# The first expert layer of a two-layer attention and mixture-of-experts kernel computed on rows sorted by expert instead of on all rows

## The chip, the cores and the metric

One core of a Trainium2 chip runs the whole program. The time is microseconds of device time per execution; the profile is one execution of the same program, taken by the hardware profiler.

## The reference

2048 tokens (32 sequences of 64) of 128 channels pass through two layers, each a cross attention of 16 heads followed by a feed-forward with 8 experts of which each token uses 2. All in fp32.

```python
x = x + xattn0(layernorm(x), ctx, ctx, ...)      # 16 heads of 8, keys and values from ctx
x = x + ffn0(layernorm(x), ...)
x = x + xattn1(layernorm(x), ctx, ctx, ...)
x = x + ffn1(layernorm(x), ...)

def ffn0(x, w_gate, w_g, w_u, w_d):              # 8 experts, hidden width 176, top 2
    top, idx = top_k(x @ w_gate, 2)
    gating = sum(one_hot(idx, 8) * softmax(top)[..., None], axis=-2)
    hidden = silu(x @ w_g[e]) * (x @ w_u[e])     # for every expert e
    return sum_e gating[e] * (hidden[e] @ w_d[e])
# ffn1: the same routing, gelu(x @ W1[e] + b1[e]) @ W2[e] + b2[e], hidden width 512
```

## The kernel before

The program is written by hand for each engine: the order of instructions on an engine is the order of the code, and engines meet only through semaphores (`wait_ge`, `then_inc`). Tokens lie in 16 row tiles of 128 (`TILES`), or 4 groups of 4 tiles (`GROUPS`, `G`). Products that need fp32 are made of three fp16 matmuls on high and low halves (`three`): ScalarE writes the high half (names ending in `_high`), VectorE or GpSimd subtracts it to get the low half (`_low`).

Stages in order of time. Setup: weights and context are loaded by SP, turned by TensorE, split; ScalarE fills the ninth column of the values (`vals`, L435 and L436), GpSimd clears the odd keys (L707) and VectorE the even ones (L864). Keys, values, queries of layer 0 follow; SP copies the keys into place (`place_keys`, L346) and TensorE waits for them by `kd0` (tiles 0 to 3) and `kd1` (the rest).

Attention (`attention(l)` on every engine) is a software pipeline of steps `t` from -3 on: in step t the scores of tile t+3 and their maxima (VectorE L1026), the exponentials of tile t+2, the turned probabilities of tile t+1, the weighed values of tile t, the output and residual of tile t-1 and the layer-norm statistics of tile t-2 are made. In layer 0 a step from 1 to 12 also splits one twelfth of the weights of the first feed-forward (`split_high` L477, `chunk0_low` L1224). While it runs SP fills 16,384 rows of a table in device memory, `sorted_rows`, with filler rows (L383 to L387).

First feed-forward before the change. Near the end of the attention rows are normalised and turned in five parts (`PARTS`), the logits ranked (`rank` L1286), and after it `routing` makes a matrix of token by expert weights, `combT`. `experts0` then computes all 8 experts for all tokens: 44 steps (`N0`) of 128 hidden columns by 512 tokens; in each TensorE makes gate and up (6 matmuls of 512 columns), spreads `combT` over the hidden columns (L1796) and adds 12 matmuls of 128 columns to a sum in PSUM; ScalarE applies SiLU (L589) and writes the high half (L593), VectorE multiplies twice (L1276, L1315), GpSimd makes the low half (L815). `residual0` adds a finished group to x and takes its statistics; GpSimd normalises it. In the same loop 8 chunks of the weights of the second feed-forward are split (`CHUNK_STEPS`; L600, and L1321 in two halves each). The projections of layer 1 follow, values and queries mixed (`VALUES_AT`).

Second feed-forward, as it is before and after. During attention 1 each row tile is normalised (L539), turned, its logits taken (`turn_row`, `row_logits`), the two experts chosen (`choose`), ranks within each expert counted by TensorE (`part_ranks`) and the row's place in `sorted_rows` found (`locate`), in five parts (`SORT_PARTS`). GpSimd scatters every row twice (`scatter` L784, 32 indirect DMAs), each expert's rows one after another. A table of 23 slot tiles (`MT`) of 256 rows says which expert and which rows each has: 5 (`MT0`) are found from the first 12 row tiles (`early_tiles`), 18 from all (`late_table`). `experts1` loads a slot tile (SP L411, four buffers), turns it (L1816, two transposes), splits it (L609, L1349), makes 12 matmuls of 256 columns and 26 of 128, GELU between them, and GpSimd stores the results by token into `expert_sums` (L835, two indirect DMAs a tile, eight buffers). When all have landed the two sums of each token are loaded (SP L415, ScalarE L652), weighed and added to x (L658, L1376, L1381) and stored.

## Time and profile before

| | us |
|---|---|
| median of 3 runs (434.42 to 437.73) | 435.37 |
| the profiled execution | 436.56 |
| its span | 434.6 |
| PE busy | 363.3 |
| DVE busy | 341.2 |
| ACT busy | 273.8 |
| POOL busy | 235.8 |

PE is TensorE, DVE VectorE, ACT ScalarE, POOL GpSimd, SP the engine whose queue issues most DMAs; PEld is TensorE's weight load; a name with q at its end (SPq, ACTq) is the engine's sequencer, where DMAs are issued. In a timeline row stand start, duration, engine, line, operation, what is written and read, how many instructions are merged, and in brackets the idle time of the engine before it with what ended it. A row of lines gives busy time, mean ns of one, and idle time before. A windows row gives for each engine the busy time in a stretch and the instructions, then the TensorE clock that was granted (1.00 is 2.4 GHz, 0.50 is 1.2 GHz) and the DMA share.

### The profile page before, as it was taken

The numbers are of one execution on the slowest core, as the hardware profiler recorded it, in microseconds if no ns is written. First come the engines' busy times: TensorE is split into PE (matmuls) and PEld (weight loads), VectorE is DVE, ScalarE is ACT, GpSimd is POOL, SyncE is SP. The second block draws the span as 40 slices with busy tenths as digits, with TensorE's granted clock in tenths as the row PEclk, the third lists the DMA queues.
The fourth block names the chain that finished last, engine by engine and source line by source line (L and its number), as shares of the span: only waits on it lengthen the run. The fifth ranks groups of instructions, "written<-read, shape, count | busy, mean of one in ns | idle before, by whom it ended". The sixth has DMA issues, their size and how long they took to land.

```text
span 434.6 us, 12797 instructions
## 1 busy us (share of the span) xinstructions
PE 363.3 (84%) x4463; PEld 260.0 (60%) x4463; DVE 341.2 (79%) x981; ACT 273.8 (63%) x593; POOL 235.8 (54%) x359
## 2 busy tenths in 40 slices
PE   3887999997499999999998899898844999999900
PEld 2553666666346666666555477676723798888900
DVE  5775699998878787988876489888776899999707
ACT  6564788887356665565565778686722666676504
POOL 7531277777525558585760144346776356666630
PEclk9997699999589999999999689898875899999965
DMA  7349797000001111110002300001113232322136
GB/s 203 72 130 286 200 381 275 4 2 4 2 0 50 50 50 50 50 50 0 2 14 44 46 2 3 3 15 39 40 38 97 68 89 83 94 83 69 46 94 226
DMA packets 30837, 33.15 MB, mean 76 GB/s; under 512 B 3908, under 2 KB 22606, under 8 KB 30776
## 3 DMA queue, kind: packets, MB, share of 16 engines
q1 hardware_dynamic: 27164, 25.84, 21.0%
q0 software_dynamic: 2496, 5.18, 3.5%
q10 hardware_dynamic: 1116, 1.31, 0.9%
q8 instruction: 38, 0.62, 0.6%
q14 instruction: 23, 0.19, 0.1%
HBM read 15.22 MB, written 15.01 MB: 70 GB/s over the span
## 4 chain that ended last, share of the span: by engine, by line
PE 54%; DVE 15%; POOL 11%; issue 9%; ACT 5%; DMA 4%; ACTq 1%; POOLq 0%; DVEq 0%; SPq 0%
PE ps L1433 11%; PE ps L1435 10%; PE ps L1434 10%; PE ps L1665 6%; PE ps L1524 4%; DVE area L1026 4%; POOL sorted_rows L792 4%; PE ps L1480 2%; PE ps L1498 2%; PE ps L1595 2%; POOL expert_sums L835 2%; POOL area L815 2%; DMA keys<-expert_sums 2%; PE ps L1796 1%; PE ps L1816 1%
## 5 line engine op out<-in xcount | busy, mean ns | idle before, releaser
L815 POOL TENSOR_TENSOR area<-area 128x512 f16<-128x512 f32 x44 | 51.0, 1158 | 42.6 <-ACT area L593 42.5
L1433 PE MATMUL ps<-w,area 128*128 128x128 f16 (+1 forms) x360 | 63.7, 219 | 0.3 <-POOL area L815 0.2
L1434 PE MATMUL ps<-w,area 128*128 128x128 f16 (+1 forms) x360 | 63.7, 219 | 0.0
L1435 PE MATMUL ps<-w,area 128*128 128x128 f16 (+1 forms) x360 | 63.7, 219 | 0.0
L835 POOL DMA_INDIRECT expert_sums<-area x46 | 46.7, 1016 | 30.7 <-ACT area L615 20.1
L1433 PE MATMUL ps<-area,w 128*128 128x512 f16 (+1 forms) x180 | 60.2, 335 | 2.5 <-DVE area L1349 0.9
L1434 PE MATMUL ps<-area,w 128*128 128x512 f16 (+1 forms) x180 | 60.0, 333 | 0.0
L1435 PE MATMUL ps<-area,w 128*128 128x512 f16 (+1 forms) x180 | 59.9, 333 | 0.0
L1026 DVE TENSOR_REDUCE area<-ps 128x8 f32<-128x512 f32 x64 | 41.2, 686 | 16.4 <-PE ps L1665 15.0
L589 ACT ACTIVATE area<-ps 128x512 f32<-128x512 f32 x44 | 26.3, 597 | 36.4 <-PE ps L1435 35.8
L639 ACT ACTIVATE area<-ps,b_now 128x256 f32<-128x256 f32 x92 | 36.1, 474 | 11.4 <-PE ps L1435 11.2
L1524 PE MATMUL ps<-ident,area 128*128 128x128 f32 x256 | 41.9, 316 | 1.0 <-ACT area L514 1.0
L1276 DVE SCALAR_TENSOR_TENSOR area<-ps,area 128x512 f32<-128x512 f32 x44 | 30.1, 683 | 14.3 <-ACT area L589 14.3
L1665 PE MATMUL ps<-keys,q_T 32*64 32x256 f16 x768 | 37.4, 300 | 2.3 <-DVE q_T L941 2.1
L1433 PEld LDWEIGHTS ps<-w,area 128*128 128x128 f16 x360 | 35.2, 98 | 6.2 <-POOL area L815 1.3
L1434 PEld LDWEIGHTS ps<-w,area 128*128 128x128 f16 x360 | 35.2, 98 | 4.8
L792 POOL DMA_INDIRECT sorted_rows<-w,area x32 | 31.7, 991 | 11.3 <-issue 9.4
L514 ACT ACTIVATE area<-ps 128x512 f32<-128x512 f32 x64 | 34.8, 599 | 3.9 <-PE ps L1595 3.3
L1435 PEld LDWEIGHTS ps<-w,area 128*128 128x128 f16 x360 | 35.2, 98 | 0.0
L1524 PEld LDWEIGHTS ps<-ident,area 128*128 128x128 f32 x256 | 33.2, 162 | 3.1 <-ACT area L514 2.5
L1369 DVE TENSOR_TENSOR area<-area 128x512 f16<-128x512 f32 x46 | 32.4, 704 | 1.6
L1315 DVE TENSOR_TENSOR area<-ps,area 128x512 f32<-128x512 f32 x44 | 30.4, 692 | 2.0 <-PE ps L1796 0.5
(241 smaller groups left out, 999.0 us busy)
## 6 DMA issues: line engine op xcount, KB each, us to landing
sorted_rows<-filler_rows SPq DMA_DIRECT2D x16, 528.0 KB, 6.4
w_stage<-in_L_ffn_W SPq DMA_DIRECT2D x8, 512.0 KB, 4.1
w<-sorted_rows SPq DMA_DIRECT2D x23, 132.0 KB
keys<-area SPq DMA_DIRECT2D x32, 48.0 KB
area<-in_ctx SPq DMA_DIRECT2D x4, 256.0 KB, 5.0
keys<-expert_sums SPq DMA_DIRECT2D x4, 256.0 KB, 5.4
keys<-expert_sums ACTq DMA_DIRECT2D x4, 256.0 KB, 6.1
out<-x_res SPq DMA_DIRECT2D x8, 128.0 KB, 1.9
```

What stands on the lines that cost most here:

```text
L514: nc.scalar.activation(probs[:, t % 2, h * HALF:(h + 1) * HALF], ps[:, 2 * (t % 2) + h, :], ACT.Exp, scale=float(HD) ** -0.5 / ASCALE ** 2 ...
L639: nc.scalar.activation(act_f[:, n % 4, f * ST:(f + 1) * ST], ps[:, n % 4, f * ST:(f + 1) * ST], ACT.Gelu, bias=b1_now[:, 2 * u + f, j:j + ...
L792: nc.gpsimd.indirect_dma_start(out=sorted_rows, out_offset=bass.IndirectOffsetOnAxis(ap=place[:, t, c:c + 1], axis=0), in_=rows32[:, t, :] ...
L815: nc.gpsimd.tensor_tensor(hid[:, n % 4, 1, :], gated[:, n % 4, :], hid[:, n % 4, 0, :], ALU.subtract).then_inc(q["lo"], 1)
L835: nc.gpsimd.indirect_dma_start(out=expert_sums, out_offset=bass.IndirectOffsetOnAxis(ap=to_row[:, j, h:h + 1], axis=0), in_=ys[j % OUTS][: ...
L1026: nc.vector.tensor_reduce(mx[:, v, h * hh:(h + 1) * hh], ps[:, 2 * v + h, :].rearrange("p (h k) -> p h k", k=SEQ), axis=AX.X, op=ALU.max). ...
L1369: nc.vector.tensor_tensor(hid1[:, n % 8, 1, :], act_f[:, n % 4, :], hid1[:, n % 8, 0, :], ALU.subtract).then_inc(q["lo"], 1)
L1433: pe.matmul(dst, lhs[0], rhs[0], start=start, stop=False, **kw)
L1434: pe.matmul(dst, lhs[0], rhs[1], start=False, stop=False, **kw)
L1435: return pe.matmul(dst, lhs[1], rhs[0], start=False, stop=stop, **kw)
L1524: mm = pe.matmul(ps[:, 4 + h, n * P:(n + 1) * P], probs[:, t % 2, c:c + P], ident[:, :], is_transpose=True, start=(n == 0), stop=(n == 3), ...
L1665: mm = pe.matmul(ps[64 * b:64 * b + 64, 2 * v + n // 2, HALF // 2 * odd:HALF // 2 * (odd + 1)].rearrange("p (j k) -> p j k", j=QUAD), q_T[ ...
```

## The change

The first feed-forward takes the path of the second. Nearly every sorting function gets the layer `l` as an argument; the two layers have tables `sorted_rows[l]` and `expert_sums[l]` of their own.

- `attention(0)` now runs the steps of `attention(1)`: statistics, `rows_normalise`, `turn_row`, `row_logits`, `choose`, `part_ranks`, `locate`, `scatter`, `last_steps`. `PARTS`, `rank`, `low`, `routing`, `combT`, `expert_rows` and `residual0` are gone. The rows of layer 0 lie where the keys were turned, so their first writers wait for `kd1`.
- The table of layer 0 isn't filled in advance. The experts lie `STRIDE` = 2304 rows apart, and SP writes 256 filler rows behind each expert's last row (`fill_ends`) between the fourth and the fifth slot load. That of layer 1 is filled by 18 DMAs instead of 16.
- `experts0` has 23 slot tiles: per tile two transposes, 12 matmuls of 256 columns, SiLU and its high half on ScalarE, gate, low half and slot arrival on VectorE (the low half is no longer GpSimd's), 12 matmuls of 128 columns, two indirect stores.
- Five of the eight weight chunks are split in it, three in steps 0 to 5 of attention 1. The bias rows of the second output are made in it too, by ScalarE and VectorE.
- The sums come back through device memory, all eight loads on SP; they are weighed and added, and only then come statistics, normalised rows, queries. Keys and values 0 to 5 are projected before.
- Setup: GpSimd fills all of `vals` and writes the ones columns later; ScalarE has no fill; the clearing of the odd keys comes after that of the value weights.

```diff
+STRIDE = SLOTS + ST
-FILLS = 16
+FILLS = 18
...
+        rows32 = [part[:, 0:TILES * ROW].rearrange("p (t r) -> p t r", r=ROW) for part in (rows0, w0_words)]
+        sums = [part[:, 0:2 * TILES * D].rearrange("p (c t d) -> p c t d", c=2, d=D) for part in (
+            area, keys[:, :, :, :].rearrange("p i j k -> p (i j k)").bitcast(F32))]
...
+        CHUNK_STEPS = (2, 6, 10, 14, 18)
+        CHUNKS_NOW = len(CHUNK_STEPS)
+        CHUNK_LOADS = (10, 14, 18, 22)
...
+            def fill_ends():
+                q = F[0]
+                sp.wait_ge(q["fill"], 1)
+                for e in range(EXPERTS):
+                    end = sp.value_load(fill_row[0:1, e:e + 1], min_val=0, max_val=EXPERTS * STRIDE - ST)
+                    sp.dma_start(sorted_rows[0][bass.ds(end, ST), :].rearrange("(p r) w -> p (r w)", p=P),
+                                 filler_rows[:, 0:2 * ROW].bitcast(U32)).then_inc(q["filled"], 16)
...
+                for j in range(MT):
+                    if l == 0 and j == LOADS:
+                        fill_ends()
+                    if j == MT0:
+                        sp.wait_ge(q["tbl"], 5)
+                        sp.wait_ge(q["sc"], 2 * 16 * (TILES - EARLY))
+                        if l == 0:
+                            sp.wait_ge(q["spare"], 16)
+                            sp.wait_ge(q["filled"], 16 * EXPERTS)
...
+            load_slots(0)
+            next_chunk(6)
+            sums_landed(0)
+            for g in range(GROUPS):
+                for c in range(2):
+                    load_sums(0, g, c)
             place_keys(1, 0)
             place_keys(1, 1)
+            next_chunk(7)
...
-            nc.scalar.activation(ninth[0], own_half[:, :].unsqueeze(1).broadcast_to(each), ACT.Copy).then_inc(s["ninth"], 1)
-            nc.scalar.activation(ninth[1], zero_eps[:, 0:1].unsqueeze(1).broadcast_to(each), ACT.Copy).then_inc(s["ninth"], 1)
...
+                for j in range(MT):
+                    act.wait_ge(q["up"], j + 1)
+                    positive_wait(act, q["gt"], j - 3)
+                    nc.scalar.activation(act_f[:, j % 4, :], ps[:, j % 2, :], ACT.Silu, scale=1 / WSCALE).then_inc(q["act"], 1)
+                    if j >= 1:
+                        gated_high(j - 1)
+                    if j + 2 < MT:
+                        slots_high(0, j + 2)
+                    if j in CHUNK_STEPS:
+                        chunk_high(CHUNK_STEPS.index(j))
+                    if j == 8:
+                        output_bias_rows()
+                    if j >= 2:
+                        weigh(0, j - 2)
...
+            act.wait_ge(F[0]["pr"], 4)
             for g in range(GROUPS):
+                weigh_second(0, g)
+                if g >= 1:
+                    turned_queries(1, g - 1)
+                if g >= 2:
+                    queries_high(1, g - 2)
...
+            last_scatters(0)
+            store_results(0)
+            for g in range(GROUPS):
+                rstds(G * g, G, G * g + 2 * TILES, g % 2 * G)
+                for t in range(G * g, G * g + G):
+                    row_normalise(1, t)
...
+                for j in range(MT):
+                    gate(j)
+                    if j + 2 < MT:
+                        arrive(0, j + 2)
+                    if j >= 1:
+                        gated_low(j - 1)
                     for h in range(2):
+                        if j - h in CHUNK_STEPS:
+                            chunk_low(CHUNK_STEPS.index(j - h), h)
+                    if j == 9:
+                        output_bias_rows()
...
+            for g in range(GROUPS):
+                add_first(0, g)
+                for h in range(2):
+                    add_second(0, g, h)
+                next_statistics(g)
+                if g >= 2:
+                    queries_low(1, g - 2)
...
+                def gate_up(j, e):
+                    pe.wait_ge(q["xs_lo"], j + 1)
+                    positive_wait(pe, q["gt"], j - 1)
+                    for n in range(2):
+                        for c in range(2):
+                            mm = three(ps[:, 2 * n + j % 2, c * ST:(c + 1) * ST], (wgu[n][c][0][:, e, 0:P], wgu[n][c][1][:, e, 0:P]),
+                                       (xs_T[:, j % 2, 0, :], xs_T[:, j % 2, 1, :]))
+                    mm.then_inc(q["up"], 1)
...
+                for j in range(MT + 2):
+                    if j < MT:
+                        gate_up(j, experts[j])
+                        if j + 2 < MT:
+                            turn(0, j + 2)
+                    if j >= 2:
+                        down(j - 2, experts[j - 2])
```

## Rows read from the trace of the kernel before

**Rows 1.** The cores view: span and mean granted clock.

```profile
core 0: 434.6 us, clock 0.900
```

**Rows 2.** Windows view, the first feed-forward: stretch, length, busy time of each engine, clock.

```profile
125.00:221.00 96.00, 94.71 (x818) 58.00 (x816) 77.63 (x131) 57.32 (x97) 61.29 (x65) 1.00 0.12 34
```

**Rows 3.** Timeline of all engines in the setup: start, duration, instruction.

```profile
6.82 2.76 ACT L436 ACTIVATE vals<-zero_eps 128x512 f16<-128x512 f32 x1
...
7.57 2.00 PE L1456 MATMUL ps<-ident,area 128*128 128x128 f32 x8 [1.57 <-DMA area<-in_ctx]
...
10.81 1.08 ACT L669 ACTIVATE ctx_T<-ps 128x512 f16<-128x512 f32 x2
```

**Rows 4.** Timelines of single engines: the marks between stages.

```profile
35.55 1.29 DVE L1026 TENSOR_REDUCE area<-ps 128x8 f32<-128x512 f32 x2 [0.54 <-PE ps L1665]
...
237.34 1.29 DVE L1026 TENSOR_REDUCE area<-ps 128x8 f32<-128x512 f32 x2 [0.60 <-PE ps L1665]
...
335.86 1.11 PE L1816 MATMUL ps<-ident,w 128*128 128x128 f32 x4 [3.40 <-DMA w<-sorted_rows]
...
354.58 0.38 PE L1816 MATMUL ps<-ident,w 128*128 128x128 f32 x2
...
402.28 0.38 PE L1816 MATMUL ps<-ident,w 128*128 128x128 f32 x2
...
419.69 1.92 SPq L415 DMA_DIRECT2D keys<-expert_sums  x4
```

**Rows 5.** Windows view, a quiet stretch of each attention.

```profile
60.00:101.00 41.00, 37.74 (x621) 26.42 (x620) 38.67 (x101) 36.26 (x82) 30.56 (x71) 1.00 0.34 123
...
255.00:273.00 18.00, 18.00 (x297) 13.38 (x293) 16.18 (x50) 15.50 (x40) 9.83 (x19) 1.00 0.01 2
```

**Rows 6.** Lines view of the whole span: busy us, mean ns of one, idle before.

```profile
L1369 DVE TENSOR_TENSOR area<-area 128x512 f16<-128x512 f32 x46 | 32.4, 704 | 1.6
...
L1276 DVE SCALAR_TENSOR_TENSOR area<-ps,area 128x512 f32<-128x512 f32 x44 | 30.1, 683 | 14.3 <-ACT area L589 14.3
...
L1321 DVE SCALAR_TENSOR_TENSOR w<-w_stage,w 128x512 f16<-128x512 f32 x16 | 14.1, 880 | 0.9 <-ACT w L600 0.6
...
L1228 DVE SCALAR_TENSOR_TENSOR w<-w 128x352 f16<-128x352 f32 x12 | 6.3, 526 | 0.2
...
L571 ACT ACTIVATE q_T<-q_T 1x1024 f32<-1x1024 f32 x1 | 1.1, 1057 | 0.0
```

**Rows 7.** Timeline of VectorE, arrival of one slot tile.

```profile
373.32 0.42 DVE L1349 TENSOR_TENSOR area<-ps,area 128x256 f16<-128x256 f32 x1
...
374.18 0.43 DVE L1367 CAST area<-area 128x512 f16<-128x512 f32 x1
```

**Rows 8.** Stores: timeline of GpSimd at the end, and lines view 346 to 402.

```profile
417.30 0.96 POOL L835 DMA_INDIRECT expert_sums<-area  x1 [0.30 <-issue]
...
L835 POOL DMA_INDIRECT expert_sums<-area x34 | 35.1, 1033 | 25.2 <-ACT area L615 17.1 <-issue 8.1
```

**Rows 9.** Timelines: adds, statistics, normalised rows, and the setup's last query chain.

```profile
424.34 1.14 DVE L1376 SCALAR_TENSOR_TENSOR x_res<-keys,area,x_res 128x128 f32<-128x128 f32 x4 [13.50 <-DMA keys<-expert_sums]
...
426.32 1.13 DVE L1376 SCALAR_TENSOR_TENSOR x_res<-keys,area,x_res 128x128 f32<-128x128 f32 x4
...
206.33 0.87 DVE L844 BATCH_NORM_STATS2 stats<-x_res 128x6 f32<-128x128 f32 x4
...
207.24 0.38 DVE L848 BATCH_NORM_AGGREGATE mv_now<-stats 128x2 f32<-128x6 f32 x4
...
224.50 0.20 POOL L721 TENSOR_TENSOR mean_var<-mv_now,zero_eps 128x4 f32<-128x4 f32 x1 [3.09 <-DVE mv_now L848]
...
225.96 1.73 POOL L732 TENSOR_SCALAR area<-x_res,mean_var,rstd 128x128 f32<-128x128 f32 x4
...
30.12 0.66 PE L1490 MATMUL ps<-ident,area 128*128 128x128 f32 x4
```

1077 lines of the change are left out of this document (450 added, 627 removed).

## Prediction

> **What bounds the kernel now.** I read the cores view first: 434.6 us at a mean granted clock of 0.9 [rows 1]. This one execution took 436.56 us with what lies around its span, 1.2 us over the median of 435.37; differences are worked out on the span and added to the median. A difference of 1% (4.4 us) is about what can be told from no change here.
>
> Then the windows by stage. In the first feed-forward (125 to 221 us) TensorE is busy 94.7 of 96 us at clock 1.00: 44 steps of 2.18 us, TensorE-bound [rows 2]. The marks cut the rest: the first score maxima come at 35.55 (first attention) and 237.34 (second), the first turned slot tile of the second feed-forward at 335.86, its eighth at 354.58, its 23rd at 402.28, the load of its sums is issued at 419.69 [rows 4]. So first maxima to first maxima is 201.8 us, and this stretch holds what is replaced. The second attention with its sort takes 98.5 us to the first slot tile; slot tiles eight to 23 come 47.7/15 = 3.18 us apart.
>
> The new first half of the kernel is a copy of this second half, so I price it there.
>
> **Setup.** ScalarE's two fills of `vals` end at 9.58, yet the context transposes ended at 9.57 and the first half of them about 8.6; ScalarE takes the context only at 10.81 [rows 3]. Without the fills that copy can follow the transposes: 10.81 - 8.6 = **-2.2 us** (bounds -1 and -3; GpSimd's longer fill and the later key clear still end before the first keys). First maxima at 35.55 - 2.2 = 33.35. The one constant table less and one more weight load on SP cost nothing: both run under the first score steps.
>
> **Sort in the first attention.** The second attention's 98.5 us already hold its row transposes, choosing, placing and 32 scatters. The first has, besides, 12 weight pieces in steps 1 to 12: 0.526 us each on VectorE [rows 6]. VectorE is busy 16.2 of 18 us of the second attention's quiet stretch, and 38.7 of 41 in the first, where the pieces are [rows 5]: with 4.5 steps of 4.0 us in the former it has 0.4 us free per step. So a piece costs between 0.13 (all of the free time is usable) and 0.526: 1.5 to 6.3 in sum. VectorE never got above 94% in the first attention, so I take 0.33 each, **4.0**. The new waits of ScalarE, GpSimd and VectorE for the placed keys (`kd1`) cost 0: TensorE's scores of tile 4 wait for the same semaphore a step earlier. First slot tile: 33.35 + 98.5 + 4.0 = 135.9.
>
> **23 slot tiles.** TensorE: against the second feed-forward a tile drops 14 of 26 matmuls of 128 columns and keeps twelve of 256: 4608 of 6400 columns, so at most 0.72 x 3.18 = 2.3 us. VectorE: gate 0.68, arrival 0.86 (373.32 to 374.18), low half 0.70 = 2.24 us [rows 6, 7], and it must wait in each tile for ScalarE's activation and slot copy; no row has this, I allow 0.4 (bounds 0 and the 0.7 of a full operation). Into tiles 6, 7, 10, 11, 14, 15, 18, 19 falls a weight half of 0.88 [rows 6], which fills that wait. GpSimd: a store lasts 0.96 and the next starts 0.30 later [rows 8], two per tile: 2.52. So VectorE sets the pace, GpSimd close behind.
>
> - First to eighth turn: 18.7 as in the second, less three down projections of 0.88 saved (2.6), plus chunk 0 (two halves, 1.8, of which 0.8 fills waits): 17.1. The eight end fills of SP go in ahead of the fifth slot load: at 1.92/4 = 0.48 us per issue [rows 4] it is 3.8 us later. The sixth load waits for the last scatters anyway; I count 0, and 3.8 if that cover fails.
> - Eighth to 23rd: 7 x 2.64 + 8 x 3.12 = 43.4; three one-partition bias copies of 1.06 on ScalarE [rows 6] behind tile 8, of which I let 1.1 through: 44.5. Lower bound the stores alone, 15 x 2.52 = 37.8; upper 15 x 2.64 + 7.0 + 3.2 = 49.8.
> - 23rd turn to the load of the sums: 17.4 in the second; 2.6 less TensorE, 0.7 more for the gate in the last chain gives 15.5, but the last results bunch and the stores queue: 16.5.
>
> Together **78.1**: sums asked for at 214.0.
>
> **A rule weighed.** The 34 stores between 346 and 402 us lasted 1033 ns in the mean against 0.96 for one alone [rows 8]: something slows them a little. At that mean the stores need 15 x 2.66 = 39.9 and stay hidden under the 44.5; if one store of each tile had to wait out one low half of VectorE (0.70) they would need 15 x 3.22 = 48.3. That is rival B. The Trainium skill (SBUF — State Buffer, "SBUF: two separate sides") has such a rule: GpSimd and a VectorE instruction with two SBUF inputs hold one port pair in turn, each for its whole instruction; by it this would be the likely course.
>
> **Sums through device memory.** From issue to the first add 419.69 to 424.34 = 4.65; the adds of a group take 1.98, statistics 0.91 + 0.38 = 1.29 [rows 9]: 4 x 3.27 = 13.1. Between them VectorE takes the first query's low half (0.7), for which ScalarE must first weigh and turn: a wait of 2.5 (bounds 0 and 4). After the last statistics GpSimd needs 224.50 to 227.69 = 3.2, and from the last row transposes to the first maxima the setup needed 30.12 to 35.55 = 5.4 [rows 4, 9]. Sum 4.65 + 13.1 + 0.7 + 2.5 + 3.2 + 5.4 = **29.6** (bounds 27 and 33). Keys and values of the second attention run under it, TensorE being idle. SP places the second keys behind the eight sum loads, early enough. New first maxima: 243.6, against 237.34: **+6.3**.
>
> **Second attention.** Three of the eight weight chunks move here: 6 halves of 0.88 in steps 0 to 5, less 0.4 free per step = 2.9, bounds 1 and 5.3; **+2.9**. Second feed-forward and output are the same code: 0.
>
> Sum: 6.3 + 2.9 = +9.2; 435.4 + 9.2 = **444.6 us**; this execution's 436.56 would be 445.8. In words: the experts get 18 us shorter (96 to 78), but the first attention grows by its sort (35.55 to 125 = 89.5 before, 102.5 after, +13) and the way to the next attention from 16 to 30 (+13).
>
> **Rivals.** (A, forecast) VectorE is the bound in attention and experts, 440 to 449, chance 0.50. (B) The stores wait for VectorE's low halves: middle stretch 48.3 instead of 44.5, 448.4. For it: 1033 against 0.96; against: the rise is only 0.07. Chance 0.13. (C) TensorE, waiting a quarter of each tile, is granted only 1.2 GHz: 4.6 us per tile, 15 x (4.6 - 3.0) = +24, 469. For: the mean clock of 0.9 says it falls somewhere [rows 1]; against: 1.00 in an attention stretch whose VectorE is 90% busy [rows 5]. Chance 0.05. (D, not slower) VectorE's added work fits in its waits: pieces 1.5, stores set the pace (37.8), chunk halves 1.0: 444.6 - 2.5 - 6.7 - 1.9 = 433.5. It decides as soon as 4.9 of these 11.1 us come true; with the shorter gather of 27 it is 430.9, faster. For: in all stretches VectorE has gaps; against: it is at 94% where the pieces are now. Chance 0.32.
>
> **Numbers.** Slower by over 1% (over 439.7): A, B, C and the end of D, 0.70. Within 1%: D, 0.20. Faster: D with a short gather, 0.10. All bounds together give 430 to 459; leaving out the ends beyond 435 and 453 leaves 8 in 10. If A holds, 440 to 449.
>
> **What would show it.** Setup: first maxima near 33.4. Sort: 12 steps of the first attention at 4.3 us each, first slot tile near 136. Experts: turned tiles 3.0 us apart, VectorE over 90% busy there, TensorE idle before the down matmuls; stores idle between pairs (if they are back to back, B or D). Sums: first add 4.7 us after the issue, adds of the next group every 3.3. Second attention: steps 0 to 5 half a us longer. Most likely to be wrong: the allowance of 0.4 per tile, the sort's 4.0, and the wait of 2.5 in the gather; a clock of 0.5 in the experts breaks the sum altogether.

## The result, and the profile after

The changed kernel takes **474.04 us** (median of 4 runs, 472.78 to 475.8) against 435.37: a ratio of 1.088, 95% interval 1.084 to 1.092. I had forecast 444.6. The direction was right, the size was not: 38.7 us more instead of 9.2, and outside the range of 435 to 453. An execution of a kernel that lay over 1.5% above its fastest counts in the medians but not in the ratios.

The cores view of the changed kernel; beside [rows 1] the granted clock has fallen from 0.9:

```profile
core 0: 472.3 us, clock 0.822
```

Its timeline at the marks that [rows 4] has for the kernel before: first score maxima of the first attention, its 16th, first, eighth and 23rd turned slot tile, load of the sums, and the same again for the second layer.

```profile
32.74 1.29 DVE L1061 TENSOR_REDUCE area<-ps 128x8 f32<-128x512 f32 x2 [0.53 <-PE ps L1651]
...
114.72 1.29 DVE L1061 TENSOR_REDUCE area<-ps 128x8 f32<-128x512 f32 x2
...
145.24 1.23 PE L1712 MATMUL ps<-ident,w 128*128 128x128 f32 x4 [3.58 <-DMA w<-sorted_rows]
...
166.26 0.38 PE L1712 MATMUL ps<-ident,w 128*128 128x128 f32 x2
...
214.43 0.38 PE L1712 MATMUL ps<-ident,w 128*128 128x128 f32 x2
...
232.39 3.67 SPq L457 DMA_DIRECT2D area<-expert_sums  x8
...
266.56 1.29 DVE L1061 TENSOR_REDUCE area<-ps 128x8 f32<-128x512 f32 x2 [1.92 <-PE ps L1651]
...
372.50 1.28 PE L1712 MATMUL ps<-ident,w 128*128 128x128 f32 x4 [1.23 <-DMA w<-sorted_rows]
...
457.04 1.76 SPq L457 DMA_DIRECT2D keys<-expert_sums  x4
```

The differences of neighbouring marks, with those of the kernel before, of the forecast, and of a kernel met below in which six places are mended:

| stage, us | before | forecast | after | six edits |
|---|---|---|---|---|
| setup, to the first maxima | 35.6 | 33.4 | 32.7 | 33.1 |
| first attention, to the first slot tile | 89.5 | 102.5 | 112.5 | 102.8 |
| first feed-forward, to the load of its sums | 96.0 | 78.1 | 87.1 | 77.8 |
| to the first maxima of the second attention | 16.3 | 29.6 | 34.2 | 31.1 |
| second attention with sort | 98.5 | 101.4 | 105.9 | 100.4 |
| second feed-forward | 83.8 | 83.8 | 84.5 | 84.2 |
| output | 14.9 | 14.9 | 15.3 | 15.1 |

(Before, the first feed-forward begins at 125 and ends at 221. Each column is one profiled execution; the last is one of 446.35 us, its kernel's median is 443.46.) Four stages are 10, 9, 4.6 and 4.5 us over the forecast. The clock comes first. The windows view of the changed kernel for the first attention behind its start up to the 16th maxima, slot tiles 8 to 23, the way to the second attention, and the score steps of that; then of the kernel before for the same stretches of its two attentions:

```profile
45.95:114.72 68.77, 59.38 (x815) 43.62 (x814) 53.63 (x177) 47.81 (x115) 27.96 (x51) 0.79 0.44 157
166.26:214.43 48.17, 40.22 (x392) 31.50 (x391) 37.46 (x96) 32.11 (x67) 31.65 (x30) 0.96 0.40 121
232.39:266.56 34.17, 15.83 (x132) 7.62 (x129) 18.61 (x64) 12.09 (x28) 13.64 (x28) 0.64 0.40 93
266.56:342.89 76.33, 65.48 (x960) 47.42 (x960) 57.70 (x182) 53.92 (x123) 29.89 (x57) 0.85 0.05 15
```

```profile
48.75:97.60 48.85, 45.77 (x754) 32.44 (x754) 45.12 (x119) 42.44 (x96) 33.71 (x77) 0.98 0.51 184
237.34:304.74 67.40, 62.71 (x960) 45.56 (x959) 53.07 (x176) 50.46 (x120) 29.73 (x57) 0.87 0.10 19
```

In the first attention TensorE's granted clock has fallen from 0.98 to 0.79, in the second only from 0.87 to 0.85: there the quiet stretch of [rows 5] had 1.00, but the whole had not. VectorE is busy 53.63 of 68.77 us in the first, 78%, so it isn't the bound that I had made of it. Two microseconds at a time, the same view shows what happens:

```profile
56.00:58.00 2.00, 0.53 (x13) 0.26 (x12) 1.48 (x4) 1.55 (x5) 0.90 (x1) 0.99 1.04 388
58.00:60.00 2.00, 1.85 (x16) 0.77 (x16) 1.32 (x5) 1.04 (x4) 0.50 (x1) 0.50 1.04 391
60.00:62.00 2.00, 2.00 (x34) 1.84 (x30) 1.59 (x4) 1.13 (x4) 0.56 (x4) 0.50 1.04 383
...
64.00:66.00 2.00, 2.00 (x30) 1.00 (x29) 1.59 (x6) 1.54 (x5) 0.20 (x1) 0.80 1.05 385
66.00:68.00 2.00, 2.00 (x37) 1.99 (x38) 1.56 (x4) 1.51 (x4) 0.87 (x4) 1.00 1.05 384
```

TensorE, at 0.99, is idle for 1.5 of 2 us (56 to 58), is granted 0.50 (1.2 GHz) for about 7 us, in which it is busy nearly throughout and hardly waits, gets 1.00 back, and is idle again at 68.7. It is a cycle of 11 to 14 us and two to three steps: six such stalls of 1.2 to 2.1 us stand between 56 and 119 us. Behind four of them the clock is 0.50 for 6.8 us, behind the other two (68.7 and 93.0) for 3.4. The stall at 70 us in the timeline:

```profile
67.63 0.49 ACT L597 ACTIVATE area<-x_res,shift,rstd 128x128 f32<-128x128 f32 x1 [0.49 <-DVE shift L1015]
67.84 1.15 POOL L824 TENSOR_TENSOR area<-area 128x512 f16<-128x512 f32 x1
68.03 0.48 ACT L535 ACTIVATE w<-w 128x352 f16<-128x352 f32 x1
68.55 0.83 DVE L1266 SCALAR_TENSOR_TENSOR w<-w 128x352 f16<-128x352 f32 x1 [0.95 <-ACT w L535]
...
69.58 0.61 DVE L1027 TENSOR_TENSOR area<-ps,area 64x128 f32<-64x128 f32 x2
70.25 0.33 PE L1671 MATMUL ps<-ident,area 128*128 128x128 f32 x1 [1.55 <-DVE area L1027]
```

ScalarE waits for VectorE's shift, normalises the row (L597), and only then makes the high half of the weight piece (L535). VectorE waits 0.95 us for that, makes the low half (L1266), and only then the weighed outputs (L1027) for which TensorE stands idle. The row normalise is new in this attention; I had priced the piece and not what it now waits behind.

### The profile page after: what moved, and what is told of

Read it like the earlier page. It is cut to its first block and busy times, and to the rows that moved or that the text cites. A ratio compares the mean times of both kernels' runs of the same rounds, so it can differ in the third digit from the quotient of the medians.

```text
span 472.3 us, 13198 instructions
## 1 busy us (share of the span) xinstructions
PE 356.2 (75%) x4253; PEld 266.5 (56%) x4253; DVE 347.1 (74%) x1135; ACT 271.9 (58%) x637; POOL 247.0 (52%) x341
## 5 line engine op out<-in xcount | busy, mean ns | idle before, releaser
L866 POOL DMA_INDIRECT expert_sums<-area x92 | 94.8, 1031 | 58.9 <-ACT area L637 30.9
L1429 PE MATMUL ps<-area,w 128*128 128x256 f16 x184 | 53.1, 289 | 7.2 <-DVE area L1284 4.8
L1429 PE MATMUL ps<-w,area 128*128 (+1 forms) x276 | 50.7, 220 | 7.6 <-DVE area L1319 7.6
L1430 PE MATMUL ps<-area,w 128*128 128x256 f16 x184 | 52.7, 286 | 0.0
L1431 PE MATMUL ps<-area,w 128*128 128x256 f16 x184 | 52.7, 286 | 0.0
L1430 PE MATMUL ps<-w,area 128*128 (+1 forms) x276 | 49.8, 219 | 0.0
L1431 PE MATMUL ps<-w,area 128*128 (+1 forms) x276 | 49.7, 218 | 0.0
L700 ACT ACTIVATE area<-ps,b_now 128x256 f32<-128x256 f32 x92 | 36.2, 475 | 11.9 <-PE ps L1431 11.8
L805 POOL TENSOR_TENSOR rstd<-mean_var,minus_half 128x1 f32<-128x1 f32 x32 | 17.8, 557 | 44.8 <-DVE mean_var L1011 44.6
L851 POOL DMA_INDIRECT sorted_rows<-area x32 | 32.2, 1008 | 11.3 <-issue 9.9
L817 POOL CAST area<-area 128x16 bf16<-128x16 f32 x32 | 6.3, 198 | 59.6 <-DVE area L1061 49.3
L573 ACT ACTIVATE area<-ps 128x512 f32<-128x512 f32 x64 | 34.9, 601 | 2.8 <-PE ps L1592 2.2
L1429 PEld LDWEIGHTS ps<-w,area 128*128 128x128 f16 (+1 forms) x276 | 26.8, 97 | 12.7 <-issue 10.2
L1651 PEld LDWEIGHTS ps<-keys,q_T 32*64 32x64 f16 x768 | 18.6, 115 | 19.5 <-issue 11.9
L1429 PEld LDWEIGHTS ps<-area,w 128*128 x184 | 18.7, 102 | 17.7 <-issue 13.9
L661 ACT ACTIVATE area<-ps 128x512 f32<-128x512 f32 x23 | 13.7, 597 | 25.9 <-PE ps L1431 25.9
```

What stands on the lines that cost most here:

```text
L573: nc.scalar.activation(probs[:, t % 2, h * HALF:(h + 1) * HALF], ps[:, 2 * (t % 2) + h, :], ACT.Exp, scale=float(HD) ** -0.5 / ASCALE ** 2 ...
L700: nc.scalar.activation(act_f[:, n % 4, f * ST:(f + 1) * ST], ps[:, n % 4, f * ST:(f + 1) * ST], ACT.Gelu, bias=b1_now[:, 2 * u + f, j:j + ...
L805: nc.gpsimd.tensor_tensor(rstd[:, j:j + 1], mv[:, j, 1:2], minus_half[:, 0:1], ALU.pow).then_inc(s["rs"], 1)
L851: nc.gpsimd.indirect_dma_start(out=sorted_rows[l], out_offset=bass.IndirectOffsetOnAxis(ap=place[:, t, c:c + 1], axis=0), in_=rows32[l][:, ...
L866: nc.gpsimd.indirect_dma_start(out=expert_sums[l], out_offset=bass.IndirectOffsetOnAxis(ap=to_row[:, j, h:h + 1], axis=0), in_=ys[j % OUTS ...
L1429: pe.matmul(dst, lhs[0], rhs[0], start=start, stop=False, **kw)
```

## Experiments

Each kernel was timed beside the kernel before. Stage times are of one profiled execution each, which can lie some us off the median given with it. Kernels that leave a stage's code alone differ in it all the same: the first attention of seven of them took 111.4 to 116.2 us, at a granted clock of 0.65 to 0.80 behind its start, the second of eight 103.6 to 109.2 (of a ninth, ends_later, 119.3). So stages are compared, with these spreads in mind, and small differences of totals are not read. Line numbers of stages are those of the changed kernel.

**The order of the pieces.** Label pieces_first.

```diff
+                    if l == 0 and t in PIECE_STEPS:
+                        split_high(PIECE_STEPS.index(t))
                     if alive(t - 2):
                         rows_normalise(l, t - 2)
-                    if l == 0 and t in PIECE_STEPS:
-                        split_high(PIECE_STEPS.index(t))
```

> The changed kernel with one order changed: in steps 1 to 12 of the first attention ScalarE makes the high half of the weight piece ahead of the row normalise instead of behind it. In the changed kernel VectorE waits 0.95 us for that high half before it makes the low half, and TensorE stands 1.6 us at the turned output behind it (56.5 to 58.2). Theory M (order and clock): this wait, not VectorE's work, makes TensorE idle, and the idle time takes its clock down; with it gone the steps go from 5.7 us towards 4.3, the granted clock of 50 to 100 us from about 0.8 to over 0.9, the last score maxima of the first attention come at 105 to 109 instead of 114.7, and the kernel takes 465 to 469 instead of 474. Theory O (occupancy): the steps are long because VectorE has more work; the order changes nothing, steps stay at 5.5 to 5.8, 473 to 475.

465.66 us, and the first attention takes 102.4 instead of 112.5, with 71.7 instead of 82.0 from the first to the 16th maxima. The same place in the timeline, and the windows up to the first step in which experts are chosen:

```profile
67.61 0.53 ACT L535 ACTIVATE w<-w 128x352 f16<-128x352 f32 x1
68.17 0.52 DVE L1266 SCALAR_TENSOR_TENSOR w<-w 128x352 f16<-128x352 f32 x1
68.25 0.50 ACT L597 ACTIVATE area<-x_res,shift,rstd 128x128 f32<-128x128 f32 x1
...
69.56 0.33 PE L1671 MATMUL ps<-ident,area 128*128 128x128 f32 x1
```

```profile
65.00:70.00 5.00, 4.88 (x82) 3.29 (x74) 4.78 (x14) 4.61 (x13) 3.06 (x5) 1.00 1.06 385
70.00:75.00 5.00, 3.51 (x65) 2.67 (x64) 4.75 (x27) 3.92 (x10) 2.07 (x4) 1.00 0.77 273
75.00:80.00 5.00, 4.38 (x52) 2.88 (x53) 3.31 (x10) 2.51 (x6) 0.96 (x3) 0.53 0.04 14
```

The wait of 0.95 us is gone, VectorE is at 96% from 65 to 70 us, and the steps there take 4.1 to 4.2 us at 1.00. Theory M holds. The first stall that is left is that of the choosing, 2.1 us at 73.5.

**The pieces by themselves.** Label pieces_after: `split_high` and `chunk0_low` of all twelve pieces stand behind the attention.

```diff
-                    if l == 0 and t in PIECE_STEPS:
-                        chunk0_low(PIECE_STEPS.index(t))
...
+                for n in range(PIECES):
+                    chunk0_low(n)
                 dve.wait_ge(q["tbl"], 3)
                 late_table(0)
```

> The changed kernel with the twelve weight pieces taken out of the steps of the first attention and made behind it, before the first slot tile, by the same engines. It prices the pieces themselves. Theory M (with the right order a piece costs about 0.33 us, with the wrong one the order costs 10 us more): 16th score maxima 67 to 68 us after the first, against 71.7 with the pieces in the right order and 82.0 in the changed kernel; the tail is 2 to 6 us longer. Theory N (it is the sort, not the pieces, that makes the steps long): 16th maxima 78 or more after the first.

The 16th maxima come 67.1 us after the first: in the right order the twelve pieces cost 71.7 - 67.1 = 4.6 us, in the order of the change 82.0 - 67.1 = 14.9. Theory M holds again. The kernel takes 465.82, as much as pieces_first, as its tail behind the 16th maxima is 7 us longer.

**The same wait put into the kernel before.** Label before_late_high.

```diff
                         nc.scalar.activation(pT[:, (t + 1) % 2, 0, 0:4, :], ps[:, 4, :].rearrange("p (a b) -> p a b", a=4),
                                              ACT.Copy).then_inc(q["p_hi"], 1)
+                    if l == 0 and t - 1 in PIECE_STEPS:
+                        split_high(PIECE_STEPS.index(t - 1))
...
-                    if l == 0 and t in PIECE_STEPS:
-                        split_high(PIECE_STEPS.index(t))
```

> The kernel before with one order changed: ScalarE makes the high half of a weight piece of the first attention behind the first copy of turned probabilities of the next step, so that VectorE, which has the low half ahead of the weighed outputs, waits for it as in the changed kernel. No sort and no added work. Theory M: TensorE idles over 1 us at the turned output again and again, its clock falls below 1.00 between 50 and 100 us, steps go from 4.06 to 5 and more, the kernel 10 to 18 us slower. Theory O (only VectorE's work counts, and that is the same): within 2 us of before.

462.25 us (456.75 to 466.6; ratio 1.050, 1.045 to 1.054): more than either theory gave, with no added work at all. Windows of it, in an execution of 465.31:

```profile
51.00:56.00 5.00, 4.21 (x76) 2.86 (x75) 2.99 (x6) 4.25 (x10) 2.05 (x4) 1.00 1.05 392
...
66.00:71.00 5.00, 4.02 (x57) 2.89 (x56) 3.04 (x9) 3.19 (x8) 2.02 (x5) 0.83 1.06 381
...
81.00:86.00 5.00, 4.57 (x49) 3.45 (x50) 2.90 (x8) 2.10 (x5) 2.55 (x7) 0.50 0.00 0
```

From 71 us on the clock stays at 0.50 until behind the 16th maxima (125.8), and the steps take 6.73 us instead of 4.06: up to the 16th maxima 88.4 us instead of 62.0. This settles that the wait and what it does to the clock are enough for the loss.

**More work for TensorE.** Label more_scores.

```diff
+                        if l == 0 and 1 <= t <= 12:
+                            for _ in range(2):
+                                scores(t + 3, v, 0)
                         scores(t + 3, v, 0).then_inc(q["s_half"], 1)
```

> The changed kernel with more work for TensorE: in steps 1 to 12 of the first attention the first half of the scores (12 matmuls, 0.53 us at the full clock) is made three times over, the last one counting; it stands right before TensorE's wait for the turned output. Theory C (the lost clock is what makes the steps long): with 1.06 us more work a step TensorE idles less than 1 us, keeps 1.00, and the steps take 5.0 to 5.3 instead of 5.7: the kernel gets 4 to 8 us faster although TensorE does more. Theory W (the waits themselves are the cost, the clock follows them at no price): TensorE's added work is hidden at best: same, or up to 12 us slower.

479.62 us, the first attention 118.7 (in an execution of 485.2, above the four others at 479.2 to 480.1): theory C's forecast fell. The stalls over 0.8 us went from six to four, but in the windows view the clock did not return for it:

```profile
66.00:72.00 6.00, 6.00 (x81) 4.33 (x81) 3.13 (x11) 2.85 (x8) 2.08 (x4) 0.50 1.05 384
72.00:78.00 6.00, 6.00 (x82) 5.05 (x78) 4.22 (x12) 3.66 (x8) 1.54 (x3) 0.50 0.31 106
78.00:84.00 6.00, 6.00 (x65) 4.36 (x58) 2.65 (x7) 3.47 (x8) 2.08 (x4) 0.50 0.01 3
84.00:90.00 6.00, 6.00 (x129) 4.63 (x126) 4.92 (x26) 4.26 (x13) 2.07 (x4) 0.94 0.02 4
```

TensorE is busy without a gap for 18 us and stays at 0.50. What brings the clock back, no run here shows; that filling this gap with work was no cure, this one does. Since the clock did not recover, it can't say what the steps would take at 1.00 with the waits left in.

**The chunk halves of the second attention.** Labels halves_first (the high half ahead of the row normalise in its step) and halves_ahead (a step earlier).

```diff
+                    if l == 1 and chunk_piece(t) is not None and chunk_piece(t) % 2 == 0:
+                        chunk_high(CHUNKS_NOW + chunk_piece(t) // 2)
                     if alive(t - 2):
                         rows_normalise(l, t - 2)
```

> The changed kernel with one order changed: in steps 0, 2 and 4 of the second attention ScalarE makes the high half of the weight chunk ahead of the row normalise. In the changed kernel VectorE waits 1.51 us for it in steps 2 and 4 and TensorE idles 2.0 us twice (291, 303.7). Theory M: these two stalls fall below 1 us, the clock stays up longer, the second attention (first maxima to first slot tile, 105.9) takes 100 to 103, the kernel 469 to 472. Theory O (the halves cost their length on VectorE wherever ScalarE's part stands): 105.5 to 106.5, 473 to 475.

Second attention 108.2, no gain, and the kernel 475.51: theory M fell here. The second kernel's edit, then a step of the first and the same of the second:

```diff
-                    if l == 1 and chunk_piece(t) is not None and chunk_piece(t) % 2 == 0:
-                        chunk_high(CHUNKS_NOW + chunk_piece(t) // 2)
+                    if l == 1 and chunk_piece(t + 1) is not None and chunk_piece(t + 1) % 2 == 0:
+                        chunk_high(CHUNKS_NOW + chunk_piece(t + 1) // 2)
```

> The changed kernel with the high halves of the three weight chunks in the second attention made a step earlier by ScalarE (steps -1, 1, 3), so that VectorE waits for none. With the order inside the step alone changed its wait fell from 1.51 to 0.50 us, but the low half then took 1.45 us beside GpSimd's subtraction of 1.15 instead of 0.69. Theory X (VectorE and GpSimd hold each other up, so only a start well ahead of GpSimd's subtraction helps): low halves take 0.7, GpSimd's operations behind them a little longer, TensorE's stalls in steps 1, 3 and 5 fall from 1.8 to 2.0 down to under 1 us, the second attention takes 100 to 103 instead of 105 to 109. Theory O (the halves simply cost their length): 105 to 109.

```profile
287.91 1.07 ACT L540 ACTIVATE w<-w_stage 128x1024 f16<-128x1024 f32 x1
288.75 1.16 POOL L824 TENSOR_TENSOR area<-area 128x512 f16<-128x512 f32 x1
289.01 1.45 DVE L1272 SCALAR_TENSOR_TENSOR w<-w_stage,w 128x512 f16<-128x512 f32 x1 [0.50 <-ACT w L540]
```

```profile
290.03 0.68 DVE L1272 SCALAR_TENSOR_TENSOR w<-w_stage,w 128x512 f16<-128x512 f32 x1
290.75 1.15 POOL L824 TENSOR_TENSOR area<-area 128x512 f16<-128x512 f32 x1
```

With the order inside the step VectorE starts 1 us sooner and then takes 1.45 us, until 0.55 us after GpSimd's subtraction is over (289.91). A step earlier it takes 0.68, GpSimd starts when it has ended, and the second attention takes **96.2 us** instead of 105.9; the kernel 468.83. Theory X holds. Four kernels with this edit and no other in the stage took 96.2, 98.0, 99.7 and 100.4, against 98.5 before and 96.7 in before_late_high, whose second attention is that of the kernel before. The rule of the Trainium skill (SBUF — State Buffer, "SBUF: two separate sides") that I had weighed for the stores, one port pair held by GpSimd or by a VectorE instruction with two SBUF inputs for the whole instruction, fits here, between GpSimd's subtraction and VectorE's low half, which both read SBUF twice: the low half ended 0.55 us behind the subtraction, its own length being 0.68.

**The low half in the first feed-forward.** Label low_first.

```diff
                     gate(j)
+                    if j >= 1:
+                        gated_low(j - 1)
                     if j + 2 < MT:
                         arrive(0, j + 2)
-                    if j >= 1:
-                        gated_low(j - 1)
```

> The changed kernel with one order changed: in the first feed-forward VectorE makes the low half of tile j-1 ahead of the arrival of slot tile j+2, not behind it. Theory L (a loop of waits: up, SiLU, gate, arrival, low half, down, next up takes two tiles, about 6.3 us): the loop loses the arrival's 1.3 us, the tiles come 2.7 to 2.9 us apart instead of 3.2, the stage from the first slot tile to the load of the sums takes 78 to 82 instead of 87.1, the kernel 465 to 469. Theory B (GpSimd's stores are held up by VectorE's low halves, 48.3 us from the eighth to the 23rd tile): the order doesn't matter, 48 us stay 48. Theory A (VectorE's sum of work): the same, since its work is the same.

The stage takes 79.8 us instead of 87.1, tiles 8 to 23 42.0 instead of 48.2 (2.80 a tile instead of 3.21); the kernel 469.16. Theory L holds, and rival B falls, since the same stores and low halves now take 42.0: the measured 48.2 is its 48.3 by chance. In the lines view of tiles 8 to 23, first of the changed kernel, then of this one, VectorE's wait at the gate (L1313) and ScalarE's before SiLU (L661) shrink:

```profile
L866 POOL DMA_INDIRECT expert_sums<-area x30 | 32.1, 1069 | 17.3 <-ACT area L637 6.6 <-issue 5.5 <-DVE area L1290 5.2
L1313 DVE SCALAR_TENSOR_TENSOR area<-ps,area 128x512 f32<-128x512 f32 x15 | 10.3, 689 | 8.7 <-ACT area L661 8.6
L661 ACT ACTIVATE area<-ps 128x512 f32<-128x512 f32 x15 | 9.0, 597 | 15.2 <-PE ps L1431 15.2
```

```profile
L866 POOL DMA_INDIRECT expert_sums<-area x30 | 29.7, 992 | 13.3 <-issue 5.1 <-ACT area L637 4.5 <-DVE area L1290 3.7
L1313 DVE SCALAR_TENSOR_TENSOR area<-ps,area 128x512 f32<-128x512 f32 x15 | 10.3, 687 | 4.8 <-ACT area L661 4.6
L661 ACT ACTIVATE area<-ps 128x512 f32<-128x512 f32 x15 | 8.9, 597 | 9.7 <-PE ps L1431 9.7
```

GpSimd itself was waiting 11.8 us for ScalarE and VectorE, so the stores held nobody up. In 7 of 15 tiles TensorE's down matmuls waited (4.7 us in all) for a low half that stood behind an arrival it had nothing to do with.

**The end fills.** Labels ends_later and filled_ahead. In the changed kernel the queue of SP shows

```profile
142.93 1.97 SPq L445 DMA_DIRECT2D w<-sorted_rows  x4
145.68 8.33 SPq L423 DMA_DIRECT2D sorted_rows<-filler_rows  x8
154.85 5.04 SPq L445 DMA_DIRECT2D w<-sorted_rows  x4
```

```diff
-                    if l == 0 and j == LOADS:
+                    if l == 0 and j == MT0:
                         fill_ends()
```

> The changed kernel with the eight end fills behind the fifth slot load instead of ahead of it. In the changed kernel the fifth load goes out at 154.85, ten us behind the fourth, and TensorE waits 2.21 us for it (157.2). Theory F (the cover of the fills failed): the fifth load goes out about ten us earlier, that wait goes, first to eighth tile takes 18.5 to 19.5 instead of 21.0, the kernel 1.5 to 2.5 us faster. Theory G (the sixth slot load, which waits for the last scatters, is then late instead): first to eighth tile stays at 20.5 to 21.3 and the wait is found at the next turned tile.

Theory F fell, and theory G had the mechanism but not the size. The fifth load goes out at 152.16, 4.2 us behind the fourth, but first to eighth tile takes 26.0 instead of 21.0, as the sixth goes out at 164.82, behind the fills. The kernel takes 482.87, more than this stage explains; why is open (the profiled execution, with 495.72 the longest of five, had a clock of 0.751). Then with the table filled in advance in place of the fills (GpSimd's first scatter waits for it):

```diff
             for n in range(FILLS):
                 r = slice(EXPERTS * STRIDE // FILLS * n, EXPERTS * STRIDE // FILLS * (n + 1))
+                sp.dma_start(sorted_rows[0][r, :].rearrange("(p m r) w -> p m (r w)", p=P, m=2), filler).then_inc(F[0]["filled"], 16)
...
-                    if l == 0 and j == LOADS:
-                        fill_ends()
```

> The changed kernel with the table of the first layer filled in advance by 18 DMAs ahead of those of the second layer, as the second's is, and without the eight end fills. The fills went out 1.1 to 1.2 us apart between the fourth and the fifth slot load (145.68 to 153.68), and putting them behind the fifth made first to eighth tile 26.0 instead of 21.0. Theory F (the fills are in the way of the slot loads): first to eighth tile takes 17.5 to 19.5, the kernel 1.5 to 4 us faster. Theory H (the earlier filler traffic collides with the key placing and the scatters): what is won there is lost in the first attention.

First to eighth tile 19.4 instead of 21.0, as theory F has it (the changed kernel and eight with other edits took 20.2 to 22.4). The total of 476.33 shows no gain; its first attention took 117.4, a little beyond the 111 to 116 of the others, so this run doesn't exclude theory H.

**The gather.** Label gather_order: all weighing first, the low halves of the queries last.

```diff
             for g in range(GROUPS):
                 weigh_second(0, g)
+            for g in range(GROUPS):
+                turned_queries(1, g)
                 if g >= 1:
-                    turned_queries(1, g - 1)
-                if g >= 2:
-                    queries_high(1, g - 2)
...
+                    queries_high(1, g - 1)
...
-                if g >= 2:
-                    queries_low(1, g - 2)
...
+            for g in range(GROUPS):
+                queries_low(1, g)
```

> The changed kernel with another order while the sums come back: ScalarE weighs all four groups before it copies any turned rows or queries, VectorE makes the four low halves of the queries after the fourth statistics. In the changed kernel the adds of the groups start at 236.85, 240.14, 243.40 and then 250.85. Theory Q (ScalarE's query work, which waits for GpSimd and TensorE, is in the way of the weighing): the fourth group starts 9.8 after the first instead of 14.0, sums' load to first maxima takes 29.5 to 31 instead of 34.2. Theory P (TensorE's query projections in fp32 at half the clock are the limit, 5 us a group): the groups are 3.3 apart but the first maxima come at 33 to 35 after the load all the same.

The adds of the fourth group start 11.2 us after the first instead of 14.0, and the first maxima come 35.3 us after the load instead of 34.2; the kernel takes 472.73. Theory Q fell, and theory P's numbers came nearly; what holds TensorE's products apart the next kernel shows. Label both_banks, on top of it:

```diff
+        def q_bank(l, g):
+            return 1 if l and g % 2 else 7
...
-                positive_wait(pe, KV["q_lo"], n)
-                pe.matmul(ps[:, 7, :], wq32[:, l, :], xT32[:, g % 2, :], start=True, stop=True).then_inc(KV["q_ps"], 1)
+                positive_wait(pe, KV["q_lo"], n - l)
+                pe.matmul(ps[:, q_bank(l, g), :], wq32[:, l, :], xT32[:, g % 2, :], start=True, stop=True).then_inc(KV["q_ps"], 1)
```

> The changed order of the gather again (all weighing first, query low halves last), and the query products of the second layer in two PSUM banks in turn instead of one. With the order alone the fourth group's adds start 11.2 instead of 14.0 after the first, and nothing came of it: 35.3 instead of 34.2 from the load of the sums to the first maxima, as TensorE's products stand 5.0 us apart, each waiting 2.1 to 2.5 for the low half of the one before. Theory R (that loop through one bank is the limit): groups of products 3.5 to 4 apart, load of the sums to first maxima 30 to 32. Theory S (half the clock alone makes it long): 33 to 35.

**27.6 us**, better than theory R's 30 to 32, the kernel 469.74: of the four products the second to the fourth start at 250.29, 253.90 and 256.36, the last two in TensorE's timeline:

```profile
253.90 1.13 PE L1496 MATMUL ps<-area,wq 128*128 128x512 f32 x2 [0.69 <-ACT area L526]
...
256.36 1.12 PE L1496 MATMUL ps<-area,wq 128*128 128x512 f32 x2 [0.69 <-ACT area L526]
```

Windows of the last part with the one bank (gather_order), and two products of the kernel all6 below, which has both edits too:

```profile
244.00:266.00 22.00, 12.43 (x42) 5.16 (x44) 8.88 (x31) 5.08 (x10) 9.58 (x20) 0.50 0.28 43
```

```profile
228.16 2.07 PE L1490 MATMUL ps<-area,wq 128*128 128x512 f32 x2 [0.69 <-ACT area L518]
...
231.97 2.07 PE L1490 MATMUL ps<-area,wq 128*128 128x512 f32 x2 [0.69 <-ACT area L518]
```

The loop through one bank kept TensorE at 56% busy and 0.50 throughout, its products 5.0 us apart. In both_banks the clock came back to 1.00 between the second product and the third; in all6 it stayed at 0.50 to the first maxima, and so the two effects can be told apart. Two banks at 0.50 bring the products to 3.6 to 3.8 us apart (228.16, 231.97, 235.59, 239.20) and the stage to 31.1, or 30.0 in early6, which theory R had; the clock on top brings the last two to 2.5 us apart and the stage to 27.6 (2.9 to 3.2 and 26.9 in early5).

**All of it.** Label all6 is the changed kernel with pieces_first, halves_ahead, low_first, filled_ahead, gather_order and both_banks.

> The changed kernel with the six edits together: pieces ahead of the row normalise, chunk high halves a step earlier, low half ahead of the arrival, table filled in advance, gather order, two query banks. Singly they gave, stage by stage, 10, 9.7, 7.3, and from the two not yet measured 2 and 3. If they add up: 474 - 32 = 442, and the first attention takes 102, the first feed-forward 76 to 78, the gather 31, the second attention 96. If a later stage gives back what an earlier one wins (the clock after an idle stretch, traffic that now falls elsewhere): 448 to 455. It beats the kernel before only below 435, which neither expects.

**443.46 us**, ratio 1.014 (1.008 to 1.019): 31 us less than the changed kernel, where the expectation had 442 for stage gains that add up. It is still slower than the kernel before. Three more edits were tried on it, the ranking of one row a step for the first ten rows (all7), with it also the weight pieces in steps -1 to 4 (all8), and these pieces alone (early6); all8b and early5 are all8 and early6 with the end fills back in place of the table filled in advance.

```diff
+                if 0 <= t - 3 < BY_ROW:
+                    rank_rows(l, t - 3, t - 2, t - 2)
...
-        PIECE_STEPS = tuple(range(1, 13))
+        PIECE_STEPS = (-1, -1, -1, 0, 0, 0, 1, 1, 2, 2, 3, 4)
```

> The six edits and a seventh, in both attentions: VectorE reads, ranks and indexes the logits of one row tile in every step (0.45 us) instead of those of four in one step (2.05 us with the rest). With the six edits the stalls that are left in the attentions are those of the steps with the choosing (TensorE idle 2.1 and 2.0 us at 73.5 and 95.4 with the pieces in order, and 1.68 at 276.5 in the kernel before, which has them in its second attention too), each followed by about 6 us at half the clock. Theory M: both attentions get 3 to 5 us shorter, 443.5 becomes 434 to 438. Theory O (VectorE's sum of work decides, and it doesn't fall): 442 to 446.

> The seven edits, and the twelve weight pieces in steps -1 to 4 of the first attention, three, three, two, two, one and one, instead of one each in steps 1 to 12. The first steps run at half the clock, and VectorE is busy there less than three quarters. Theory M: the pieces cost nothing there, and VectorE's 4.6 us a step falls below TensorE's 4.0 to 4.1 later: the first attention takes 94 to 98 instead of 102.8, the kernel 430 to 435. Rival: three pieces in a row ahead of the weighed outputs (1.6 us) make stalls of their own and prolong the cold start: no gain over the seven edits.

> As the one with eight edits, but with the end fills of the changed kernel in place of the table filled in advance. Theory F: 1 to 2 us slower in the first eight tiles. Theory H (9.5 MB of filler traffic more in the first attention slow scatters and key placing): as fast or faster in sum.

> The six edits (443.5) without the ranking by row, with the twelve weight pieces in steps -1 to 4 of the first attention (three, three, two, two, one, one). With the ranking by row and these pieces the first attention had its first stalls already in steps 1 to 4. Theory M: the clock is lost once per stall whatever the stall's length, so pieces bunched into the cold start cost one stall at most and spare the later steps: first attention 97 to 100 instead of 102.8, the kernel 438 to 441. Rival: they set off a second cold stretch at 50 to 60 us: 102 to 106, the kernel 443 to 448.

> As early6, but with the end fills of the changed kernel instead of the table filled in advance. First to eighth tile 20 to 21.5 instead of 18. Theory F: 2 to 3 us slower than early6; Theory H (the filler traffic slows the first attention): the same or faster.

all7: 456.59, both attentions longer, 107.1 and 104.1. Theory M's forecast fell: in place of stalls of 2.1, 2.0 and 1.7 us (all6: 74.0, 95.9, 107.7) there are four of 1.5 to 1.6 (61.0, 73.3, 100.3, 111.8). That the rank work of a step, 0.45 us, and the piece are together more than VectorE's free time is the likely reason, not tested by itself. all8 (459.41, where 430 to 435 was expected) and all8b (454.41) have the same ranking. early6: 443.01, first attention 101.2 (forecast 97 to 100); early5: 442.53. So the pieces bunched in the first steps win little in the total, and none of these beats the kernel before. Nor does the table filled in advance change the total. In the two pairs it wins in the first eight tiles (17.1 against 20.0 in early6 and early5, 17.3 against 21.5 in all8 and all8b) and loses between the load of the sums and the first maxima (30.0 against 26.9, 29.7 against 27.4). The first attentions, 101.2 against 106.4 and 106.9 against 106.1, do not bear out theory H. Why the gather is longer is open; in early6 its products ran at 0.50, in early5 the last three at 1.00.

## Why the prediction was wrong, step by step

- **Setup**, -2.2 forecast, -2.8 measured: right, within the bounds. ScalarE takes the context at 8.04 instead of 10.81; 0.7 of that is that its transposes started sooner (6.83 instead of 7.57), which I had not forecast.
- **Sort in the first attention**, 102.5 forecast, 112.5 measured. The term of 4.0 us for twelve pieces was right as a price of work: 4.6, and 102.4 for the stage once the order is mended. The step that failed is the reckoning that VectorE "has 0.4 us free per step": I took busy time alone and left out that ScalarE's new row normalise stands between VectorE and the high half it waits for. That wait, not VectorE's work, made TensorE idle, and behind each such stall its clock fell to 0.50. Up to the 16th maxima the changed kernel has five such stalls and, from 50 us on, 27.2 us at 0.50, pieces_first two and 10.2; the 10.3 us between the kernels are 3.4 us for each stall. If TensorE does half as much at 0.50, 17 us more of it are 8.5 of these 10.3 us, an upper estimate of the clock's part. 3.4 us is no fixed price: before_late_high lost 26.3 us with three stalls over 0.8 us and smaller waits. My "what would show it" had 12 steps at 4.3; in the changed kernel they took 3.9 to 6.8.
- **The clock.** I named it only as rival C, for the experts, at 0.05, and argued against it by an attention stretch with 1.00. That stretch has TensorE busy 100% [rows 5]: it was TensorE-bound at 4.0 us a step, and I took its 1.00 for a property of the stage. Rival C as I put it (1.2 GHz in the experts, 469) didn't come either: slot tiles 8 to 23 had 0.96.
- **23 slot tiles**, 78.1 forecast, 87.1 measured. For tiles 8 to 23 I had 44.5: 41.7 us of work of VectorE and bias copies, and 2.8 of waits, 0.4 a tile where no weight half fills it. Measured were 37.5 busy and 10.7 idle, together 48.2. The allowance for the waits failed, at 0.7 a tile; the work was over-sized, so that the miss looks smaller than it is (a weight half took 0.68 here, not 0.88). Cause of the waits: the order gate, arrival, low half; with it mended 36.1 busy and 5.9 idle, 0.4 a tile, together 42.0. First to eighth tile added 3.9 us to the miss (next point), the end of the stage 1.5. Rival B, with nearly the measured number, was the wrong mechanism.
- **End fills**, counted at 0 "and 3.8 if that cover fails". It failed, and the price was mis-sized: eight in 8.33 us, 1.04 each and not the 0.48 of a sums load. Each first reads its address into a register: the four slot loads whose addresses were read beforehand went out 0.54 apart (142.93 to 144.56), and behind the fills, where each reads its own, 1.18 (157.20 to 160.75). The fifth slot load went out 10.3 us behind the fourth, and TensorE waited 2.21 us for it. First to eighth tile took 21.0 instead of 17.1; without the fills 19.4, and in the kernels with more of the edits 17.1 to 18.0.
- **Gather**, 29.6 forecast, 34.2 measured. First add 4.5 us after the load (4.65 forecast), groups 3.26 and 3.29 apart (3.27): right. The first failing step is the 2.5 us wait, which was 4.2 between the third and fourth group; but mending it gave nothing. The step that counted is the 5.4 us "from the last row transposes to the first maxima": it was a time for one group at 1.00, and here four products stood 4.6 to 5.4 us apart, three of them at 0.50, and each but the first waited 2.1 us for the low half of the one before in the same PSUM bank.
- **Second attention**, +2.9 forecast, +7.4 measured. I had counted the halves at 0.88 and no wait. The step that failed is the same 0.4 us free per step: VectorE waited 0.8, 1.5 and 1.5 us for ScalarE's high half of 1.04 us, once then for GpSimd too, and TensorE stood idle 1.8 to 2.0 us each time. Up to the 16th maxima the stage took 76.3 us instead of 67.4 at almost the same clock (0.85 and 0.87), and 67.1 at 0.95 in halves_ahead; how much of the gain is the clock's these runs don't tell. Without the waits the halves cost between nothing and 3.7 us (96.2 to 100.4 in four kernels, against 98.5 and 96.7), so the 2.9 may have been right as a price of work.
- **Second feed-forward**: 0 forecast, +0.7 measured.

In sum the forecast of 444.6 is near the time of a kernel that has this work without these waits: all6 takes 443.5. Part of that nearness is luck: all6 fills its table another way, still has stalls of 1.7 to 2.1 us in the first attention, and its tiles 8 to 23 take 42.1 where I had 44.5, the rest of that stage 35.6 where I had 33.6. What was missing was to ask, for every instruction added to an in-order engine, what it waits for and who stands behind it.

## What to carry to other kernels

- Price an added operation by its place: who must finish before it, and which engine waits for the instruction behind it. Here two engines that wait for each other twice in a step cost more than the operation: 14.9 us in one order, 4.6 in the other.
- A stretch at full clock is no evidence that the clock holds when its busiest engine gets gaps. Where TensorE is the bound, a stall has to be priced with what the rows show behind one: here 3.4 us in the mean of one pair of kernels, and 26.3 us for three in another.
- Spreading work evenly over the steps wasn't better than bunching it: all7, with four stalls of 1.5 us in the first attention, was slower than all6, with three of 1.7 to 2.1.

## What the runs showed of the hardware

- TensorE at 0.50 stayed there for 18 us while busy without a gap (more_scores), and in before_late_high from 71 to 125.8 us, at about 90% busy; in the changed kernel it came back after 3.4 or 6.8 us. The condition stays open.
- VectorE's low half (two inputs in SBUF) beside GpSimd's subtraction took 1.45 us instead of 0.68, and a 128x352 one 0.83 instead of 0.52: it ended 0.55 and 0.39 us behind the end of GpSimd's instruction. GpSimd's indirect stores, on the other hand, lasted 1069 ns in the mean of tiles 8 to 23 beside 992 with the other order, so little of this is seen between them and VectorE.
- DMAs of SP whose address is read just before went out 1.1 to 1.2 us apart, those with addresses read beforehand 0.54.
- One fp32 product group of the queries (two matmuls of 512 columns) followed the next at 5.0 us through one PSUM bank at 0.50, at 3.6 to 3.8 through two, and at 2.5 to 3.2 through two at 1.00.
